# Tokens, attention and last stage in one block, token statistics by groups between the attention steps

## The chip, the cores and the metric

The kernel runs on one core of one Trainium2 chip. Times are device microseconds of one execution; the span of a profile is the time from its first to its last instruction.

## The reference

Three parts follow one another. A graph network makes tokens: three layers over 64 x 64 frames of 75 nodes, then a mean over the nodes. The tokens are joined with 32 text rows per batch, normalised and passed through one attention head with a residual. Then 30 rounds of a small feed-forward step, again with a residual.

```python
h = tok_ref(x, A, W0, ..., v2)                 # 64 batches x 64 tokens x 64
h = concatenate([h, txt], axis=1)              # 64 x 96 x 64
h = h + attn(layernorm(h), Wq, bq, Wk, bk, Wv, bv)
h = h + ffn(layernorm(h), ln_w, ln_b, W, b)    # 30 rounds of the step below

def step(h):
    h = h + 0.01 * tanh(h)
    h = h * sigmoid(h)
    h = layernorm(h) * ln_w + ln_b
    return einsum('bsc,dc->bsd', h, W) + b
```

The `layernorm` outside has no weights: (x - mean) / sqrt(var + 1e-5).

## The kernel before

The program is a row of blocks. Within a block each of the five engines has its own instruction stream, ordered by semaphores; between blocks all engines meet.

`setup` loads parameters and x and prepares constants. `tokenise` runs 205 iterations of five frames in four quarters and leaves the node means in `pooledT`; its last instruction is the VectorE reduction of L700, and SP's queue fetches one iteration's input two iterations ahead (`fetch`, L127).

`fuse` has two blocks. The first is `tokens` (L782). SP loads the text into rows 64 to 95 of `h` (L821). ScalarE issues six loads of weights (L828 to L831), after VectorE has cleared `w4` (L845). VectorE clears further constants (L846 to L851), waits for the text, folds the layer-norm weights into the feed-forward matrix (`fold_weights`, L858 to L872; two small matmuls, L909 and L910, belong to it), and then finishes eight groups of eight batches (`finish`): an add of the bias row from PSUM to `h` (L877) and one statistics instruction per batch (L883). TensorE makes the tokens of a group with eight matmuls (L917) into one of two PSUM banks, so a group waits for the finish of the group two before. After the eighth group the statistics of all 64 batches become a mean and an inverse root together (L894 to L933, with one square root on ScalarE, L833).

The second block holds `attention` and `feed_forward`. Attention has 16 groups of four batches in a pipeline of 20 steps. In step t, in this order:

- TensorE: probabilities times values of group t-4 (L1049), scores of t-2 (L1059), transposes of the probabilities of t-3 (L1068), query, key and value of t-1 (L1077, L1081), transposes of the normalised rows `hn` of t (L1089).
- VectorE: scaled result h2 of t-4 (L1127), maximum of t-2 (L1133), denominator of t-3 (L1137), difference to the maximum `dif` of t-2 (L1144), values of t-1 (L1150), reciprocal of t-3 (L1156).
- GpSimd: centring `hc` (L1028) and scaling `hn` (L1033) of t, one buffer each, then the residual add of t-4 (L1037).
- ScalarE copies between PSUM and SBUF and computes Exp (L1117).

Steps 4 to 9 are a loop, the others are written out. SP stores h2 by groups and reads it back in six chunks of 128 x 512. From step 10 on the engines also prepare the first four chunks for the last stage: statistics on VectorE (`STATS_AT`, L1345, L1348), the inverse root as a power on GpSimd (L1253, called in the same step), centring on GpSimd (`CENTRE_AT`, L1257), scaling on VectorE (`SCALE_AT`, L1357). Chunks 4 and 5 are prepared on VectorE and GpSimd while the last stage opens.

The last stage is software-pipelined over chunks: Tanh and Silu on ScalarE, the update y = x + 0.01 tanh(x), statistics, a power on GpSimd (L1281), scaling `gn` on VectorE (L1394), transposes (L1338) and matmuls (L1323, L1325, L1330) on TensorE.

Of the kernel before, what the change touches and what calls it, by code (L numbers as in the profile page):

```python
# [18 lines left out]
F32 = mybir.dt.float32  # L19
F16 = mybir.dt.float16  # L20
BF16 = mybir.dt.bfloat16
# [60 lines left out]
def build(nc, x_v, txt, AT, A, W0T, W1, W2, par01, par1, par2, weights, out):  # L82
# [10 lines left out]
    with ctx:  # L93
# [14 lines left out]
        pooledT = sb("pooledT", [P, QUART, QF])  # L108
        z_stored = [(sem(f"z_stored_by_sync{k}"), sem(f"z_stored_by_pool{k}")) for k in range(ZK)]
        zst_loaded = [sem(f"z_static_loaded{i}") for i in range(2)]  # L110

        with nc.sbuf_tensor("zp", [P, ZK, 2, 2, PAIRS * HC], F16) as zp:

            setup(nc, ps, x_v, AT, A, W0T, W1, W2, par01, par1, par2, zs, zp, zst, z_stored, zst_loaded,
                  AThi, ATlo, abar, W0K, W1hi, W1lo, W1s, negb1, W2s, b2row, ident)
            tokenise(nc, ps, zs, zst, z_stored, zst_loaded, pooledT, AThi, ATlo, abar, W0K, W1hi, W1lo, W1s, negb1)
        fuse(nc, ps, pooledT, h2_dram, txt, weights, W2s, b2row, ident, out)
# [14 lines left out]
def setup(nc, ps, x_v, AT, A, W0T, W1, W2, par01, par1, par2, zs, zp, zst, z_stored, zst_loaded,  # L132
          AThi, ATlo, abar, W0K, W1hi, W1lo, W1s, negb1, W2s, b2row, ident):

    with ExitStack() as ctx:
# [85 lines left out]
        with nc.Block() as block:  # L221
# [78 lines left out]
            def _(pool):  # L300
# [8 lines left out]
                pool.memset(zst[:], 1.0).then_inc(zst_clear, 1)  # L309
                pool.wait_ge(max_ready, 1)  # L310
# [167 lines left out]
def tokenise(nc, ps, zs, zst, z_stored, zst_loaded, pooledT, AThi, ATlo, abar, W0K, W1hi, W1lo, W1s, negb1):  # L478

    with ExitStack() as ctx:  # L480
# [55 lines left out]
        with nc.Block() as block:  # L536
            @block.sync
            def _(sp):
# [9 lines left out]
                steps(sp, body)  # L548

# [179 lines left out]
def fuse(nc, ps, pooledT, h2_dram, txt, weights, W2s, b2row, ident, out):  # L729

    with ExitStack() as keep:
        def kept(name, shape, dt=F32):
            return keep.enter_context(nc.sbuf_tensor(name, shape, dt))


        w4 = kept("w4", [P, 4, P])
        wq, wk, wv, wf = (w4[:, i, :] for i in range(4))
        wcol = kept("wcol", [P, 4])
        wrow = kept("wrow", [P, 2, D])
# [3 lines left out]
        brow = kept("brow", [P, FW], BF16)  # L743
        h2r = kept("h2r", [P, FCH, FW])
        h2_loaded = keep.enter_context(nc.semaphore("h2_loaded"))
        h = kept("h", [S, B, D])
        mean = kept("mean", [S, B])
        rstd = kept("rstd", [S, B])

        tokens(nc, ps, pooledT, txt, weights, W2s, b2row, ident, w4, wcol, wrow,  # L750
               pct, ones, brow, h, mean, rstd)
        with nc.Block() as block:
            prepare, last_pass = feed_forward(nc, keep, ps, h2r, h2_loaded, ident, wf, pct, ones, brow, out)
# [7 lines left out]
            @block.gpsimd  # L761
            def _(pool):
                attend["gpsimd"](pool, prepare["gpsimd"])
# [8 lines left out]
            def _(act):  # L772
                attend["scalar"](act)
# [3 lines left out]
            def _(dve):  # L777
                attend["vector"](dve, prepare["vector"])
# [3 lines left out]
def tokens(nc, ps, pooledT, txt, weights, W2s, b2row, ident, w4, wcol, wrow,  # L782
           pct, ones, brow, h, mean, rstd):

    W4, w_cols, w_rows = weights
    wf, ln_w, ln_b, bf = w4[:, 3, :], wcol[:, 2:3], wcol[:, 3:4], wrow[:, 1, :]
    v_ = nc.vector
    NT = FRAMES // P
    TG = 4
    BG = 8  # L790
    frames = pooledT[:].rearrange("p q f -> p (q f)")
    with ExitStack() as ctx:
        def sb(name, shape, dt=F32):
            return ctx.enter_context(nc.sbuf_tensor(name, shape, dt))

        def sem(name):
            return ctx.enter_context(nc.semaphore(name))

        halves = sb("halves", [P, P])
        wfT = sb("wfT", [D, D])  # L800
        lbx = sb("lbx", [D, P])
        bres = sb("bres", [P, 2, D])
        bpart = sb("bias_part", [P, D], BF16)
        bs = sb("bn_parts_h", [S, B, 6])
        st = sb("st", [S, 6, B])

        w_clear = sem("w_clear")
        w_loaded = sem("w_loaded")
        txt_loaded = sem("txt_loaded")
        chain = sem("vector_chain2")  # L810
        tok_ready = sem("tok_ready")
        tok_done = sem("tok_done")
        wl_ready = sem("wl_ready")
        mean_ready = sem("mean_ready")
        var_ready = sem("var_ready2")
        root_ready = sem("root_ready2")

        with nc.Block() as block:
            @block.sync
            def _(sp):  # L820
                sp.dma_start(h[T:S], txt.rearrange("b s d -> s b d")).then_inc(txt_loaded, 16)  # L821

            @block.scalar
            def _(act):
                act.wait_ge(w_clear, 1)
                for i in range(2):
                    half = slice(D * i, D * i + D)
                    act.dma_start(w4[half, :, half], W4).then_inc(w_loaded, 16)  # L828
                    act.dma_start(wcol[half, :], w_cols).then_inc(w_loaded, 16)
                act.dma_start(wfT[:], W4[:, 3, :]).then_inc(w_loaded, 16)  # L830
                act.dma_start(wrow[:].rearrange("p i d -> p (i d)"), w_rows.partition_broadcast(P)).then_inc(w_loaded, 16)  # L831
                act.wait_ge(var_ready, 1)
                nc.scalar.activation(st[:, 2, :], st[:, 1, :], ACT.Sqrt).then_inc(root_ready, 1)  # L833

            @block.vector
            def _(dve):
                done = [0]

                def link(ins):
# [611 lines left out]
```

## Time and profile before

| | |
|---|---|
| median of 3 runs | 1688.97 us (1688.37 to 1690.54) |
| the profiled execution | 1689.59 us |
| its span | 1687.8 us |
| busy: TensorE / VectorE / ScalarE / GpSimd | 1570.6 / 1408.3 / 1170.3 / 1348.5 us |
| mean granted TensorE clock | 0.985 of full speed |
| token loop ends | about 1218 us |
| tokens block | 1218 to 1248 us |
| attention | 1248 to 1308 us |
| last stage | to 1681 us, then the last stores |

DVE is VectorE, ACT ScalarE, POOL GpSimd, PE TensorE (PEld its weight loads). Busy times are sums over the span; engines overlap. A granted clock of 1.00 is 2.4 GHz, 0.50 is 1.2 GHz.

### The profile page before, as it was taken

The numbers are of one execution on the slowest core, as the hardware profiler recorded it, in microseconds if no ns is written. First come the engines' busy times: TensorE is split into PE (matmuls) and PEld (weight loads), VectorE is DVE, ScalarE is ACT, GpSimd is POOL, SyncE is SP. The second block draws the span as 40 slices with busy tenths as digits, with TensorE's granted clock in tenths as the row PEclk, the third lists the DMA queues.
The fourth block names the chain that finished last, engine by engine and source line by source line (L and its number), as shares of the span: only waits on it lengthen the run. The fifth ranks groups of instructions, "written<-read, shape, count | busy, mean of one in ns | idle before, by whom it ended". The sixth has DMA issues, their size and how long they took to land. (4 is left out here: it accounts for less than half of the span.)

```text
span 1687.8 us, 64798 instructions
## 1 busy us (share of the span) xinstructions
PE 1570.6 (93%) x22603; PEld 1125.7 (67%) x22603; DVE 1408.3 (83%) x3354; ACT 1170.3 (69%) x2706; POOL 1348.5 (80%) x1500
## 2 busy tenths in 40 slices
PE   8599999999999999999999999999858699999999
PEld 8466666666666666666666666666557588888887
DVE  6388888888888888888888888888767899999998
ACT  3377777777777777777777777777525688888886
POOL 2388888888888888888888888888727788888887
PEclk9999999999999999999999999999979799999999
DMA  5200000000000000000000000000102000000001
GB/s 116 87 7 7 6 7 7 6 7 6 7 6 7 7 6 7 6 7 7 7 7 6 7 6 7 7 6 7 19 5 57 17 0 0 0 0 0 0 0 38
DMA packets 21670, 21.66 MB, mean 13 GB/s; under 512 B 12254, under 2 KB 19342, under 8 KB 21271
## 3 DMA queue, kind: packets, MB, share of 16 engines
q1 hardware_dynamic: 18554, 19.07, 4.3%
q0 software_dynamic: 1120, 1.44, 0.3%
q10 hardware_dynamic: 1972, 0.86, 0.3%
q8 instruction: 13, 0.21, 0.1%
q14 instruction: 11, 0.09, 0.0%
HBM read 14.43 MB, written 6.92 MB: 13 GB/s over the span
## 5 line engine op out<-in xcount | busy, mean ns | idle before, releaser
L693 DVE SCALAR_TENSOR_TENSOR y<-ps,negb,abar 128x375 f32<-128x375 f32 x820 | 477.4, 603 | 129.6 <-PE ps L595 125.2
L649 POOL TENSOR_TENSOR y0lo<-y_whole,y0hi 128x384 f16<-128x384 f32 x410 | 375.0, 915 | 146.1 <-ACT y_whole L625 132.4
L580 PE MATMUL ps<-AThi,y0hi 64*128 64x150 f16 (+1 forms) x4920 | 435.9, 217 | 6.4 <-POOL y0lo L649 4.0
L580 PE MATMUL ps<-AThi,y0lo 64*128 64x150 f16 (+1 forms) x4920 | 436.5, 215 | 0.0
L580 PE MATMUL ps<-ATlo,y0hi 64*128 64x150 f16 (+1 forms) x4920 | 436.2, 215 | 0.0
L624 ACT ACTIVATE y0hi<-ps 128x384 f16<-128x384 f32 x410 | 201.7, 492 | 328.9 <-PE ps L563 324.5
L658 POOL TENSOR_TENSOR y<-y 128x370 f32<-128x370 f32 x410 | 398.1, 971 | 8.3 <-DVE y L693 1.8
L1281 POOL TENSOR_TENSOR rs<-var,expo 128x8 f32<-128x8 f32 x180 | 313.9, 1754 | 50.7 <-DVE var L1348 50.7
L599 PE MATMUL ps<-z_whole,W1s 128*128 128x375 f32 x820 | 340.7, 497 | 0.1
L682 DVE SCALAR_TENSOR_TENSOR y0lo<-ps,y0hi 128x384 f16<-128x384 f32 x410 | 226.5, 553 | 75.2 <-ACT y0hi L626 75.2
L580 PEld LDWEIGHTS ps<-AThi,y0hi 64*128 64x128 f16 x4920 | 259.2, 94 | 21.6 <-issue 11.6
L580 PEld LDWEIGHTS ps<-ATlo,y0hi 64*128 64x128 f16 x4920 | 262.8, 96 | 0.0
L580 PEld LDWEIGHTS ps<-AThi,y0lo 64*128 64x128 f16 x4920 | 260.1, 94 | 0.0
L660 POOL TENSOR_TENSOR y<-y 128x190 f32<-128x190 f32 x410 | 218.0, 532 | 32.2
L687 DVE TENSOR_TENSOR z1lo<-ps,z1hi 128x375 f16<-128x375 f32 x410 | 220.6, 538 | 1.9 <-ACT z1hi L630 1.9
L631 ACT ACTIVATE z_whole<-ps 128x375 f32<-128x375 f32 x410 | 211.4, 516 | 0.0
L630 ACT ACTIVATE z1hi<-ps 128x375 f16<-128x375 f32 x410 | 207.3, 506 | 3.8 <-PE ps L580 3.7
L626 ACT ACTIVATE y0hi<-ps 128x384 f16<-128x384 f32 x410 | 205.2, 500 | 0.0
L625 ACT ACTIVATE y_whole<-ps 128x384 f32<-128x384 f32 x410 | 199.7, 487 | 0.0
L1325 PEld LDWEIGHTS ps<-w,gT 128*128 128x128 f32 x1440 | 190.4, 193 | 6.9
L1325 PE MATMUL ps<-w,gT 128*128 128x128 f32 x1440 | 190.9, 276 | 0.0
L599 PEld LDWEIGHTS ps<-z_whole,W1s 128*128 128x128 f32 x820 | 132.5, 189 | 83.2 <-issue 70.2
(199 smaller groups left out, 2413.6 us busy)
## 6 DMA issues: line engine op xcount, KB each, us to landing
z_static<-z_rows SPq DMA_DIRECT2D x410, 18.0 KB
xs<-in_x_v SPq DMA_DIRECT2D x5, 720.7 KB, 9.1
z_rows<-zp SPq DMA_DIRECT2D x10, 240.0 KB
h_rows<-h SPq DMA_DIRECT2D x16, 96.0 KB, 1.9
h2r<-h_rows SPq DMA_DIRECT2D x6, 256.0 KB, 2.7
out<-h2r SPq DMA_DIRECT2D x6, 256.0 KB, 2.3
z_rows<-zp POOLq DMA_DIRECT2D x5, 240.0 KB, 3.5
h<-in_txt SPq DMA_DIRECT2D x1, 512.0 KB, 4.9
```

Of the source, the lines that this page charges most:

```text
L580: last = nc.tensor.matmul(ps[:, Z1B + 2 * p + j, f0 * V:f0 * V + w], y[rows, par, p, t * C:(t + 1) * C], a[rows, BAND0[t]:BAND0[t] + w], s ...
L599: nc.tensor.matmul(ps[:, Y1B + 1, 0:GV], W1s[:], z1f[:, par, p, :], start=True, stop=True).then_inc(y1_ready[1], 1)
L630: nc.scalar.activation(z1hi[:, par, p, :], ps[:, Z1B + 2 * p, 0:GV], ACT.Identity).then_inc(z1hi_done, 1)
L631: nc.scalar.activation(z1f[:, par, p, :], ps[:, Z1B + 2 * p + 1, 0:GV], ACT.Identity).then_inc(z1f_done, 1)
L649: nc.gpsimd.tensor_tensor(y0lo[:, par, p, 0:HC], y0f[:, p, :], y0hi[:, par, p, 0:HC], ALU.subtract).then_inc(y0lo_by_pool, 1)
L658: nc.gpsimd.tensor_tensor(y[:, :, U1:2 * U1], y[:, :, U1:2 * U1], y[:, :, 0:U1], ALU.add).then_inc(halved, 1)
L660: nc.gpsimd.tensor_tensor(y[:, :, U2:V], y[:, :, U2:V], y[:, :, U1:U2], ALU.add).then_inc(quartered, 1)
L682: nc.vector.scalar_tensor_tensor(y0lo[:, par, p, HC:2 * HC], ps[:, Y0B + 1, 0:HC], 0.0, y0hi[:, par, p, HC:2 * HC], ALU.max, ALU.subtract) ...
L687: nc.vector.tensor_tensor(z1lo[:, par, p, :], ps[:, Z1B + 2 * p, 0:GV], z1hi[:, par, p, :], ALU.subtract).then_inc(z1lo_done, 1)
L693: nc.vector.scalar_tensor_tensor(y1[:, par, 2 * p + i].rearrange("p f v -> p (f v)"), ps[:, Y1B + i, 0:GV], negb1[:, 0:1], abar[:].rearran ...
L1281: nc.gpsimd.tensor_tensor(rs[:, b, :], var[:, b, :], expo[:], ALU.pow).then_inc(rs_done, 1)
L1325: last = nc.tensor.matmul(ps[:, cn, j * P:(j + 1) * P], gT[:, b, j * P:(j + 1) * P], wf, start=False, stop=(j == CP - 1), skip_group_check ...
```

## The change

- The loads of text and weights are issued by SP in the block of the token loop, behind its last fetch (`load_last`). `w4` is cleared by GpSimd in `setup`. `w4`, `wcol`, `wrow`, `wfT` and `h` are allocated for the whole program.
- The block of `tokens` is gone. Its work is handed to the attention block as pieces. TensorE makes groups 0, 1 and 2 ahead, into banks 7, 6 and 5, and the others into bank 7 in front of steps 2, 4, 6, 8 and 10. VectorE finishes groups 0 and 1, folds the weights, and finishes groups 2 to 7 in front of steps 1, 3, 5, 7, 9 and 11. GpSimd takes the power -0.5 of group g in front of step 2g. Constants are cleared by GpSimd; `pct` is made by ScalarE.
- The statistics of a group are four instructions for two batches each in place of eight. The variance stays 64 times as large as before, so the inverse root is 8 times too small; ScalarE multiplies the query, key and value weights by 8 once.
- The 20 steps of attention are all written out.
- The preparation of the last stage moves: statistics in steps 10, 12, 14, 17 (10, 13, 15, 18 before), roots a step later than their statistics, scaling in steps 13, 15, 17 and the fourth in the opening of the last stage; chunks 4 and 5 in its steps 2 and 4 (0 and 2 before).

```diff
+        def load_last(eng):
+            W4, w_cols, w_rows = weights
+            eng.dma_start(h[T:S], txt.rearrange("b s d -> s b d")).then_inc(txt_loaded, 16)
+            eng.wait_ge(w_clear, 1)
+            for i in range(2):
+                half = slice(D * i, D * i + D)
+                eng.dma_start(w4[half, :, half], W4).then_inc(w_loaded, 16)
+                eng.dma_start(wcol[half, :], w_cols).then_inc(w_loaded, 16)
+            eng.dma_start(wfT[:], W4[:, 3, :]).then_inc(w_loaded, 16)
+            eng.dma_start(wrow[:].rearrange("p i d -> p (i d)"), w_rows.partition_broadcast(P)).then_inc(w_loaded, 16)
...
                 pool.memset(zst[:], 1.0).then_inc(zst_clear, 1)
+                pool.memset(w4[:], 0.0).then_inc(w_clear, 1)
                 pool.wait_ge(max_ready, 1)
...
                 steps(sp, body)
+                load_last(sp)
...
+        pairs = kept("bn_pairs_h", [S, B // 2, 6])
+        mean = pairs[:].rearrange("p j (i k) -> p (j i) k", i=2)[:, :, 1]
-        tokens(nc, ps, pooledT, txt, weights, W2s, b2row, ident, w4, wcol, wrow,
-               pct, ones, brow, h, mean, rstd)
...
             def _(pe):
-                attend["tensor"](pe)
+                token["tensor"](pe)
+                attend["tensor"](pe, token["tensor_step"])
                 last_pass["tensor"](pe)
...
+    AHEAD = 3
+    MEANS = (4, 3)
+    def bank(g):
+        return 7 - g if g < AHEAD else 7
+    def make_tokens(pe, g):
+        if g >= AHEAD:
+            pe.wait_ge(tok_done, g if g > AHEAD else 1)
+        for j in range(BG):
+            b = g * BG + j
+            last = nc.tensor.matmul(ps[0:T, bank(g), j * D:(j + 1) * D], frames[:, b * T:(b + 1) * T],
+                                    W2s[:], start=True, stop=True)
+        last.then_inc(tok_ready, 1)
+    def tensor(pe):
+        for g in range(AHEAD):
+            make_tokens(pe, g)
+        pe.wait_ge(wl_ready, 1)
+        pe.wait_ge(filled, 2)
+        nc.tensor.matmul(ps[:, MEANS[0], 0:P], halves[:], wf, start=True, stop=True).then_inc(mean_ready, 1)
+        nc.tensor.matmul(ps[:, MEANS[1], 0:D], lbx[:], wfT[:], start=True, stop=True).then_inc(mean_ready, 1)
+        pe.wait_ge(w_eight, 1)
+    def tensor_step(pe, t):
+        if t == 2:
+            pe.wait_ge(folded, 1)
+            pe.wait_ge(pct_made, 1)
+        if t == 3:
+            pe.wait_ge(tok_done, AHEAD)
+        if t % 2 == 0 and 2 <= t and t // 2 + 2 < NT:
+            make_tokens(pe, t // 2 + 2)
+    def scalar(act):
+        nc.scalar.activation(pct[:], ident[:], ACT.Identity, scale=0.01).then_inc(pct_made, 1)
+        act.wait_ge(w_loaded, NW * 16)
+        nc.scalar.activation(w4[:, 0:3, :], w4[:, 0:3, :], ACT.Identity, scale=D ** 0.5).then_inc(w_eight, 1)
+    def gpsimd(pool):
+        pool.memset(expo[:], -0.5)
+        pool.memset(ones[:], 1.0)
+        pool.memset(brow[:], 0.0)
+        pool.memset(halves[:], 0.0).then_inc(halves_clear, 1)
...
+    def gpsimd_step(pool, t):
+        if t % 2 == 0 and t // 2 < NT:
+            g = t // 2
+            pool.wait_ge(var_ready, g + 1)
+            nc.gpsimd.tensor_tensor(rstd[:, batches(g)], var[:, batches(g)], expo[0:S, 0:BG], ALU.pow).then_inc(rstd_ready, 1)
+            pool.wait_ge(rstd_ready, g + 1)
+    def finish(dve, g):
+        dve.wait_ge(tok_ready, g + 1)
+        v_.tensor_tensor(h[0:T, batches(g), :], ps[0:T, bank(g), :].rearrange("p (b d) -> p b d", b=BG),
+                         b2row[0:T].rearrange("p (one d) -> p one d", one=1).to_broadcast([T, BG, D]),
+                         ALU.add).then_inc(tok_done, 1)
+        dve.wait_ge(tok_done, g + 1)
+        for j in range(g * BG // 2, (g + 1) * BG // 2):
+            last = v_.bn_stats(pairs[:, j, :], h[:, 2 * j:2 * j + 2, :].rearrange("p i d -> p d i"))
+        last.then_inc(bn_made, 1)
+        dve.wait_ge(bn_made, g + 1)
+        v_.tensor_scalar(var[:, batches(g)], square[:, batches(g)], D * EPS, None, ALU.add).then_inc(var_ready, 1)
...
+        dve.wait_ge(txt_loaded, 16)
+        for g in range(2):
+            finish(dve, g)
+        fold_weights()
+    def vector_step(dve, t):
+        if t % 2 == 1 and (t + 3) // 2 < NT:
+            finish(dve, (t + 3) // 2)
...
-    def steps(eng, body, after=None):
-        for t in range(4):
-            body(t, lambda lag, t=t: t - lag >= 0)
-        with eng.Fori(4, 10) as t:
-            body(t, lambda lag: True)
-        for t in range(10, NG + 4):
-            body(t, lambda lag, t=t: t - lag < NG)
+    def steps(eng, body, before=None, after=None):
+        for t in range(NG + 4):
+            if before:
+                before(eng, t)
+            body(t, lambda lag, t=t: 0 <= t - lag < NG)
             if after:
                 after(eng, t)
...
-    STATS_AT, CENTRE_AT, SCALE_AT = (10, 13, 15, 18), (11, 14, 16, 18), (12, 15, 17, 19)
+    STATS_AT, ROOT_AT, CENTRE_AT, SCALE_AT = (10, 12, 14, 17), (11, 13, 15, 18), (12, 14, 16, 18), (13, 15, 17)
     EARLY = len(STATS_AT)
-    LATE_STATS_AT, LATE_SCALE_AT = (0, 2), (1, 4)
+    LATE_STATS_AT, LATE_SCALE_AT = (2, 4), (1, 3, 5)
...
-        if t in STATS_AT:
-            pool_root(pool, STATS_AT.index(t))
+        if t in ROOT_AT:
+            pool_root(pool, ROOT_AT.index(t))
...
-                c = EARLY + LATE_SCALE_AT.index(s)
-                dve.wait_ge(centred[1], c - EARLY + 1)
+                c = EARLY - 1 + LATE_SCALE_AT.index(s)
+                if c < EARLY:
+                    dve.wait_ge(centred[0], c + 1)
+                else:
+                    dve.wait_ge(centred[1], c - EARLY + 1)
                 first_scale(dve, c)
```

## Rows read from the trace of the kernel before

**Rows 1.** Busy us of PE, PEld, DVE, ACT, POOL by stage; granted clock.

```profile
1256.00:1277.00 21.00, 19.53 (x203) 18.40 (x199) 15.44 (x40) 13.73 (x35) 12.17 (x20) 1.00 0.18 37
1277.00:1300.00 23.00, 19.58 (x202) 17.95 (x201) 17.84 (x54) 12.14 (x33) 16.66 (x22) 1.00 0.26 61
1300.00:1324.00 24.00, 7.58 (x54) 6.13 (x54) 20.27 (x62) 11.53 (x21) 17.33 (x13) 0.60 0.19 43
...
1400.00:1600.00 200.00, 200.00 (x1399) 167.49 (x1397) 190.00 (x650) 160.66 (x300) 173.11 (x101) 1.00 0.00 0
```

**Rows 2.** Waits, 1215 to 1325: who <- whom, us, times, longest.

```profile
ACT st L833 <- DVE st L901: 34.2, 1, 34.2
...
POOL rs L1253 <- DVE var L1348: 8.1, 5, 2.2
...
DVE w L858 <- DMA wrow<-in_w_rows: 5.5, 1, 5.5
```

**Rows 3.** Timeline: start us, us, engine, line, instruction, count, [idle before <-releaser].

```profile
33.02 0.42 POOL L311 PARTITION_ALL_REDUCE mxa<-mx  x1 [23.40 <-DVE mx L387]
...
1189.12 7.02 SPq L127 DMA_DIRECT2D z_static<-z_rows  x4
...
1217.52 0.55 DVE L700 TENSOR_REDUCE pooledT<-y 128x20 f32<-128x380 f32 x1 [1.75 <-POOL y L660]
...
1218.39 2.71 PE L917 MATMUL ps<-W2s,pooledT 128*64 128x64 f32 x32 [3.29 <-PEq L536]
...
1225.63 0.29 DVE L858 TENSOR_SCALAR w<-w,wcol 128x128 f32<-128x128 f32 x1 [5.50 <-DMA wrow<-in_w_rows]
...
1227.05 0.69 PE L910 MATMUL ps<-wfT,lbx 64*128 64x64 f32 x2
...
1230.25 0.68 DVE L877 TENSOR_TENSOR h<-ps,b2row 64x512 f32<-64x512 f32 x1
...
1239.60 1.15 PE L917 MATMUL ps<-W2s,pooledT 128*64 128x64 f32 x16 [0.58 <-DVE h L877]
...
1249.36 0.58 PE L1089 MATMUL ps<-ident,hn 96*128 96x96 f32 x2 [8.61 <-POOL hn L1033]
```

**Rows 4.** Groups of instructions, whole span: busy us, mean ns.

```profile
L1345 DVE BATCH_NORM_STATS2 bn_pairs<-h2r 128x6 f32<-128x128 f32 x24 | 5.2, 274 | 0.0
...
L1348 DVE TENSOR_SCALAR var<-bn_pairs 128x8 f32<-128x8 f32 x186 | 31.9, 171 | 6.4
```

**Rows 5.** One source line: duration ns min/median/max, first and last start.

```profile
L1253 POOL TENSOR_TENSOR rs<-var,expo x6: 1643/1670/2017, 1281.4 to 1318.2; 128x8 f32<-128x8 f32 x6
```

**Rows 6.** Groups of instructions in attention steps, 1260 to 1277 us.

```profile
L1037 POOL TENSOR_TENSOR h<-h x6 | 4.3, 724 | 4.3 <-DVE h L1127 4.3
...
L1033 POOL TENSOR_TENSOR hn<-hc,rstd 96x256 f32<-96x256 f32 x6 | 3.7, 609 | 4.2 <-PE ps L1089 4.2
...
L1077 PE MATMUL ps<-hT,w 128*128 128x192 f32 x24 | 5.1, 333 | 0.0
```

**Rows 7.** Timeline, TensorE in attention: step 1; transposes of steps 3, 10, 15.

```profile
1250.36 1.65 PE L1077 MATMUL ps<-hT,w 128*128 128x192 f32 x4 [0.42 <-ACT hT L1110]
...
1259.15 0.33 PE L1089 MATMUL ps<-ident,hn 96*128 96x96 f32 x2
...
1279.59 0.33 PE L1089 MATMUL ps<-ident,hn 96*128 96x96 f32 x2
...
1298.08 0.36 PE L1089 MATMUL ps<-ident,hn 96*128 96x96 f32 x2
```

**Rows 8.** Timeline: a disturbed centring, the last h2, the last stage's opening.

```profile
1288.00 1.17 POOL L1028 TENSOR_TENSOR hc<-h,mean 96x256 f32<-96x256 f32 x1
...
1308.05 0.42 DVE L1127 TENSOR_TENSOR h<-ps,inv 96x256 f32<-96x256 f32 x1 [1.01 <-PE ps L1049]
...
1320.19 0.70 DVE L1394 TENSOR_TENSOR gn<-g,rs 128x512 f32<-128x512 f32 x1
...
1326.79 1.06 PE L1338 MATMUL ps<-ident,gn 128*128 128x128 f32 x4
```

More of the change, by code:

```diff
@@ L777, in _, with tokens @@
             def _(dve):
-                attend["vector"](dve, prepare["vector"])
+                token["vector"](dve)
+                attend["vector"](dve, token["vector_step"], prepare["vector"])
                 last_pass["vector"](dve)
-def tokens(nc, ps, pooledT, txt, weights, W2s, b2row, ident, w4, wcol, wrow,
-           pct, ones, brow, h, mean, rstd):
-    W4, w_cols, w_rows = weights
+def tokens(nc, ctx, ps, pooledT, W2s, b2row, ident, w4, wcol, wrow, wfT, w_loaded, txt_loaded,
+           pct, ones, brow, expo, h, pairs, rstd):
@@ L927, in inverse_root, with sb, sem @@
-def inverse_root(link, v_, root, x, out, tmp):
-    link(v_.reciprocal(out, root))
-    link(v_.tensor_tensor(tmp, out, out, ALU.mult))
-    link(v_.tensor_tensor(tmp, tmp, x, ALU.mult))
-    link(v_.tensor_scalar(tmp, tmp, -0.5, 1.5, ALU.mult, ALU.add))
-    link(v_.tensor_tensor(out, out, tmp, ALU.mult))
+    square = pairs[:].rearrange("p j (i k) -> p (j i) k", i=2)[:, :, 2]
+    def sb(name, shape, dt=F32):
+        return ctx.enter_context(nc.sbuf_tensor(name, shape, dt))
+    def sem(name):
+        return ctx.enter_context(nc.semaphore(name))
@@ new lines, in tokens @@
+    halves = sb("halves", [P, P])
+    lbx = sb("lbx", [D, P])
+    bres = sb("bres", [P, 2, D])
+    bpart = sb("bias_part", [P, D], BF16)
+    var = sb("var64_h", [S, B])
+    chain = sem("vector_chain2")
+    halves_clear = sem("halves_clear")
+    filled = sem("constants_filled")
+    pct_made = sem("pct_made")
+    tok_ready = sem("tok_ready")
+    tok_done = sem("tok_done")
+    bn_made = sem("bn_made_h")
+    var_ready = sem("var_ready2")
+    rstd_ready = sem("rstd_ready")
+    wl_ready = sem("wl_ready")
@@ new lines, in tokens, with batches @@
+    mean_ready = sem("mean_ready")
+    w_eight = sem("w_times_eight")
+    folded = sem("folded")
+    def bank(g):
+        return 7 - g if g < AHEAD else 7
+    def batches(g):
+        return slice(g * BG, (g + 1) * BG)
+    def make_tokens(pe, g):
[6 more added lines that the diff above has]
+        last.then_inc(tok_ready, 1)
@@ new lines, in vector, with link, fold_weights @@
+    def vector(dve):
+        done = [0]
+        def link(ins):
+            done[0] += 1
+            ins.then_inc(chain, 1)
+            dve.wait_ge(chain, done[0])
+        def fold_weights():
+            dve.wait_ge(w_loaded, NW * 16)
+            link(v_.tensor_scalar(wf, wf, ln_w, D ** 0.5, ALU.mult, ALU.mult))
+            v_.tensor_copy(lbx[:], ln_b[0:D].to_broadcast([D, P])).then_inc(wl_ready, 1)
+            dve.wait_ge(mean_ready, 1)
+            link(v_.tensor_tensor(wf, wf, ps[:, MEANS[0], 0:P], ALU.subtract))
+            dve.wait_ge(mean_ready, 2)
+            link(v_.tensor_tensor(bres[:, 0, :], bf, ps[:, MEANS[1], 0:D], ALU.add))
+            dve.wait_ge(filled, 2)
+            for i in range(3):
+                r = slice(32 * i, 32 * i + 1)
+                last = v_.tensor_copy(brow[r, :].rearrange("p (r d) -> p r d", d=D),
+                                      bres[r, i % 2, :].rearrange("p (one d) -> p one d", one=1).to_broadcast([1, FR, D]))
+                if i < 2:
+                    link(v_.tensor_copy(bpart[:], bres[:, i % 2, :]))
+                    link(v_.tensor_tensor(bres[:, 1 - i % 2, :], bres[:, i % 2, :], bpart[:], ALU.subtract))
+            last.then_inc(folded, 1)
+        dve.wait_ge(txt_loaded, 16)
+        for g in range(2):
+            finish(dve, g)
+        fold_weights()
@@ L1091, in body @@
                 last.then_inc(hT_ready, 1)
-        steps(pe, body)
+        steps(pe, body, token)
     def scalar(act):
```

173 lines of the change are left out of this document (35 added, 138 removed).

## The prediction

> **What bounds the kernel now.** I read the busy time by stage first, then the waits around the changed part, then the timeline from the end of the token loop to the last stage, then the cost of single instructions. The stages show that the last stage is TensorE's alone: 200.00 us busy of 200 [rows 1]. The change touches no instruction of it after its opening, and none of the token loop before its last reduction, which ends at 1217.52 + 0.55 = 1218.07 [rows 3]. So whatever is won or lost between 1218 and about 1327 us arrives at the end one for one, and nothing else does.
>
> That stretch has three parts. From 1218.39 (first token matmul) to 1249.36 (first transposes of attention) TensorE mostly waits [rows 3]: for the weights, on which VectorE stands 5.5 us [rows 2]; for their folding, which VectorE does ahead of any token, 1225.63 to 1230.25 [rows 3]; for eight groups of tokens and one inverse root over all of them. From 1249.36 to 1298 attention runs; TensorE is busy 19.53 of 21 us at full clock [rows 1], and a step takes (1279.59 - 1259.15) / 7 = 2.92 us [rows 7]. From 1300 to 1324 TensorE is busy 7.58 of 24 us at a mean granted clock of 0.60 [rows 1], because the last stage opens on VectorE and GpSimd.
>
> **The change part by part.** I follow it on the clock of the old trace. Durations are rows; the schedule laid out of them, with 0.05 to 0.1 us for a wait between engines, is my estimate.
>
> *Loads.* SP's last fetch of the loop is issued by 1189.12 + 7.02 = 1196.1 [rows 3]; the seven loads follow it. Before, the six weight loads were there 1225.63 - 1218.39 = 7.2 us after the block began, so now text and weights lie in SBUF some 10 us ahead of need and the 5.5 us go; without that cover they return whole. Clearing w4 moves to GpSimd in the setup, which then waits 23.40 us anyhow [rows 3]. The small clears took VectorE at most 1225.63 - 5.50 - 1218.39 = 1.7 us; on GpSimd, at up to twice that, they end by 1221.8, about when the first variance is due (below): 0 to 0.2, I take 0. ScalarE's two scalings fall where it waited 34.2 us [rows 2].
>
> *Front, +24.1 us.* TensorE makes groups 0 to 2 at once. Sixteen matmuls took 2.71 us, so 1.36 a group: ready at 1219.75, 1221.1 and 1222.45 [rows 3]. One "finish" is the add, 0.68 [rows 3], four statistics over two batches each, 5.2 / 24 x 4 = 0.87, and a variance, 0.17 [rows 4]: 1.75 with its waits, done at 1221.55 and 1223.2. Folding keeps its 4.6 us, to 1227.8, and finish 2 comes behind it, to 1229.4. On GpSimd the power of group 0 runs from 1221.6 to 1223.3 (1.64 at best, 1.67 at the median [rows 5]); hc and hn, same shape, 0.61 each [rows 6], end at 1224.65. TensorE has first to do the two matmuls on the folded weights, which ended 1227.05 + 0.69 - 1225.63 = 2.1 us after the folding began [rows 3], now at 1225.25. First transposes: 1225.25 instead of 1249.36.
>
> *Steps 0 to 3, -1.3.* The projections of step 1 took 1.65 us [rows 7], against 5.1 / 6 = 0.85 in later steps [rows 6]: the clock was then at 1.2 GHz, its low level. I leave that, and add token group 3 in step 2: 1.0 at full clock (1.15 from first to last end [rows 3]) to 1.36. The wait for the first Exp stays. If the low level lasts through step 2, another 2 us go. Step 3 ends at 1236.65 against 1259.48: 22.8 ahead.
>
> *Steps 4 to 10, -4.1.* Even steps carry a token group (four of them, 4 to 7): 2.92 + 1.0 on TensorE. Odd steps carry a finish on VectorE. In a pair of steps VectorE has 2 x 2.15 (15.44 us in 21 / 2.92 steps [rows 1]) + 1.75 = 6.05 us of 6.85, GpSimd 2 x (0.61 + 0.61 + 0.72) [rows 6] + 1.65 = 5.55. The order holds too: queued behind a finish on VectorE are the step's h2, top, den and dif, and dif still ends about 0.7 us before the scores that wait for it. So only TensorE pays: 4 x 1.03. End of step 10: 1261.3 against 1279.9. The steps that were a loop are now written out, as step 10 was before, which came at the same 2.92: nothing.
>
> *Steps 11 to 15, -2.25.* Before, the early roots of the last stage made GpSimd wait for variances that VectorE had yet to make, 8.1 us over five [rows 2]; two of these hit attention and are most of what its steps 11 to 15 took over 5 x 2.92: 1298.26 - 1279.92 = 18.35 [rows 7]. Now a root stands a step after its statistics and that wait goes. But the roots of steps 11 and 13 run straight into the token powers of steps 12 and 14: 2 x 1.65 + 1.94 = 5.25 us of GpSimd, and a centring besides, against 2.92. What is late next is hn, and TensorE's transposes with it. VectorE adds 0.75 in step 12, where finish 7 follows the first statistics and no token group on TensorE covers it. I lay out 2.9, 6.0, 3.0, 5.5 and 3.2 us: 20.6. End of step 15: 1281.9.
>
> *Tail, +1.1.* Statistics 2 leave step 15, which puts VectorE's chain 0.95 us earlier; a scale and statistics in step 17 weigh about what they did in 17 and 18. Last h2 done: 1291.0 against 1308.47 [rows 8].
>
> *Opening of the last stage, +2.4.* Scale 3, statistics 4 and their centring stood ahead of the first update of x0; now they come behind it. By the same durations the first gn is 8.1 us after the last h2 (1320.19 - 1308.47 = 11.7 before), but from there to the third transposes, where TensorE takes over, it is 7.8 (1326.79 - 1320.19 = 6.6 before [rows 8]), since statistics 4 and 5 and a scale that waits for its Tanh lie between. Third transposes: 1306.9.
>
> Sum: 24.1 - 1.3 - 4.1 - 2.25 + 1.1 + 2.4 = 19.95; by the two ends, 1326.79 - 1306.9 = 19.9. The profiled execution took 1689.59 us, 1.79 more than its span of 1687.8 and 0.6 more than the median of the runs, 1688.97. Off the median: 1669.1 us.
>
> **Weighed against a rule.** Statistics and powers now run side by side. The old trace shows what that can do: hc took 1.17 us at 1288.00 [rows 8], against 0.61, while VectorE ran a scale with two SBUF inputs (L1357), and the slowest root took 2.02, median 1.67 [rows 5]. In the new loop the add reads PSUM and one SBUF row, a statistics instruction one SBUF tile, so the sum has 1.65 and 0.61. The Trainium skill (GPSIMD Engine Reference, Key points) says that GpSimd shares its SBUF interfaces with VectorE and contends with VectorE instructions that have two SBUF inputs or run in a two-port mode. Read narrowly, that spares the finish; if the finish counts after all, rival 1 follows.
>
> **Rivals.** 1: GpSimd becomes the bound of attention. With powers at 2.02 and hc at 1.17 an even step needs 2.02 + 1.17 + 0.61 + 0.72 + 0.2 = 4.7 us against TensorE's 3.95: 0.8 x 4, and 2 x 0.37 + 0.56 = 1.3 in each double step, 5.8 in all: 1674.9. For it speak those two collisions; against it, that most roots took 1.65 beside a busy VectorE.
>
> 2: More is won. If the token matmuls lift the clock before step 1, its projections save 0.8 and its values in proportion 0.4; if GpSimd runs far enough ahead for steps 11 to 15 to cost what they did, 2.25 more: 1665.6. For it, that TensorE now has work in nearly every microsecond from 1218; against it, that hn is a single buffer.
>
> 3: The loads still gate. Landing after 1223 would bring back up to 5.5: 1674.6. Against it the 1196.1.
>
> 4, the other side: TensorE does not get its full clock in attention. It was granted 1.00 with 19.53 of 21 us busy and 0.60 with 7.58 of 24 [rows 1], and the new loop has stalls of 2 to 3 us. A step of 2.92 can become 5.85; seven such steps eat the gain, thirteen give 1669.1 + 38 = 1707. Against it: from 1277 to 1300, with stalls near 2 us, the clock stayed at 1.00 [rows 1].
>
> **How the numbers follow.** Forecast (1666.5 to 1673) 0.62; rival 1, 0.17; rival 2, 0.12; rival 3, 0.03; rival 4, 0.06, of which 0.02 with about seven slow steps, no change, and 0.04 with more. A change of 0.2%, 3.4 us, is about what this measurement can tell. Faster 0.94, same 0.02, slower 0.04. The range holds the forecast, rival 1 whole and most of rival 2: 1664 to 1677.
>
> **What would show it.** Right: no VectorE wait for weights; first transposes about 7 us after the loop's last reduction; steps of 3.9 and 2.9 us by turns; two stalls of TensorE on hn, in steps 12 and 14, over 2 us each with what queues behind; the third transposes of the last stage 16 us after the last h2; its 200 of 200 unchanged. Wrong: a finish over 2 us, powers near 2 us in the loop, TensorE waiting for tok_done or folded, or a granted clock under 1.00 after step 3.

## The result, and the profile after

The changed kernel takes 1669.57 us (median of 4 runs, 1668.63 to 1670.29) against 1689.49 (4 runs, 1688.37 to 1690.54): ratio 0.9882, 95% interval 0.9865 to 0.9899. I had forecast 1669.1. Run again beside other kernels it took 1669.85 against 1689.26, ratio 0.9881 (0.9862 to 0.9901). The total is as forecast. Its terms are not all so, and that is what the experiments are about.

The lines of the kernel moved: the last reduction L700 is now L722, the tokens L917 L855, the add L877 L902, the fold L858 L925, attention's transposes L1089 L1107, h2 L1127 L1145, the first scale L1357 L1370, the update of x0 L1383 L1399, gn L1394 L1410, the last stage's transposes L1338 L1351. The front, on VectorE, in the timeline of the kernel after (start, duration, engine, line; in brackets the idle time before and what ended it), to set beside [rows 3]:

```profile
1215.68 0.55 DVE L722 TENSOR_REDUCE pooledT<-y 128x20 f32<-128x380 f32 x1 [1.76 <-POOL y L682]
1218.60 0.68 DVE L902 TENSOR_TENSOR h<-ps,b2row 64x512 f32<-64x512 f32 x1 [2.38 <-PE ps L855]
...
1222.02 0.28 DVE L925 TENSOR_SCALAR w<-w,wcol 128x128 f32<-128x128 f32 x1
...
1226.42 0.42 DVE L935 CAST brow<-bres 1x512 bf16<-1x512 f32 x1
1226.88 0.68 DVE L902 TENSOR_TENSOR h<-ps,b2row 64x512 f32<-64x512 f32 x1
```

No wait for weights is left. Two finishes take 1.7 us each, the fold 4.8. TensorE in the same part and over two steps, to set beside [rows 7]:

```profile
1216.55 5.35 PE L855 MATMUL ps<-W2s,pooledT 128*64 128x64 f32 x48 [3.30 <-PEq L557]
...
1223.87 0.36 PE L1107 MATMUL ps<-ident,hn 96*128 96x96 f32 x2 [0.41 <-POOL hn L1051]
...
1226.90 1.15 PE L855 MATMUL ps<-W2s,pooledT 128*64 128x64 f32 x16 [0.74 <-DVE brow L935]
...
1234.72 0.33 PE L1107 MATMUL ps<-ident,hn 96*128 96x96 f32 x2
1234.98 1.15 PE L855 MATMUL ps<-W2s,pooledT 128*64 128x64 f32 x16
...
1238.88 0.33 PE L1107 MATMUL ps<-ident,hn 96*128 96x96 f32 x2
...
1241.81 0.33 PE L1107 MATMUL ps<-ident,hn 96*128 96x96 f32 x2
```

The first transposes come 8.19 us after the start of the last reduction (31.84 before), an even step takes 1238.88 - 1234.72 = 4.16 us and an odd one 2.93. The opening of the last stage, to set beside [rows 8], first on VectorE, then on GpSimd, then TensorE's third transposes:

```profile
1289.89 0.42 DVE L1145 TENSOR_TENSOR h<-ps,inv 96x256 f32<-96x256 f32 x1 [0.38 <-PE ps L1067]
1290.60 2.23 DVE L1399 SCALAR_TENSOR_TENSOR x<-th,x 128x512 f32<-128x512 f32 x1 [0.28 <-ACT th L1311]
1292.74 1.21 DVE L1370 SCALAR_TENSOR_TENSOR x<-x,rs 128x512 f32<-128x512 f32 x1
1293.88 0.68 DVE L1399 SCALAR_TENSOR_TENSOR x<-th,x 128x512 f32<-128x512 f32 x1
...
1300.55 0.69 DVE L1410 TENSOR_TENSOR gn<-g,rs 128x512 f32<-128x512 f32 x1
```

```profile
1291.22 1.05 POOL L1273 TENSOR_TENSOR x<-h2r,bn_pairs 128x512 f32<-128x512 f32 x1
1292.23 1.17 POOL L1055 TENSOR_TENSOR h<-h 96x256 f32<-96x256 f32 x1
```

```profile
1308.75 1.12 PE L1351 MATMUL ps<-ident,gn 128*128 128x128 f32 x4 [0.42 <-DVE gn L1410]
```

The first update of x0 took 2.23 us, the next 0.68. The table gives the gain over the profiled execution of before by stretches, for two profiled executions of the changed kernel (spans 1667.5 and 1668.3 against 1687.8). Positive is faster; pct is the constant 0.01 times the identity by which TensorE adds a tanh:

| stretch | forecast | first | second |
|---|---|---|---|
| start to last reduction of the token loop | 0 | 1.84 | 0.89 |
| to the first transposes of attention | 24.1 | 23.65 | 23.65 |
| to those of step 3 | -1.3 | -1.06 | -1.06 |
| to those of step 10 | -4.1 | -4.98 | -4.98 |
| to those of step 15 | -2.25 | -2.40 | -2.72 |
| to the end of the last h2 | 1.1 | 1.11 | 0.94 |
| to the first pct matmul of the last stage (opening) | 2.4 | -0.36 | 0.30 |
| to its last pct matmul | 0 | 2.51 | 2.45 |
| to the end | 0 | -0.01 | -0.01 |

Attention is right within 1 us a row. The opening is wrong by 2.1 to 2.8 us, and the last stage's loop and the start gave 3.3 to 4.4 that I had not forecast. The prediction took the opening to the third transposes: they came 18.44 and 18.31 us after the last h2, against 18.32 before and 15.9 forecast. In the experiments I compare the stretch from the start of the last reduction to the last pct matmul, called **the stretch**: 456.04 us before, 437.57 and 437.46 after.

### The profile page after: what moved, and what is told of

It is laid out like the page before. It is cut to its first block and busy times, and to the rows that moved or that the text cites. A ratio compares the mean times of both kernels' runs of the same rounds, so it can differ in the third digit from the quotient of the medians.

```text
span 1667.5 us, 64566 instructions
## 1 busy us (share of the span) xinstructions
PE 1566.6 (94%) x22603; PEld 1123.6 (67%) x22603; DVE 1407.9 (84%) x3311; ACT 1168.7 (70%) x2707; POOL 1365.7 (82%) x1514
## 5 line engine op out<-in xcount | busy, mean ns | idle before, releaser
L1338 PEld LDWEIGHTS ps<-w,gT 128*128 128x128 f32 x1440 | 190.6, 193 | 6.9
L1338 PE MATMUL ps<-w,gT 128*128 128x128 f32 x1440 | 191.1, 276 | 0.0
```

Of the source, the lines that this page charges most:

```text
L1338: last = nc.tensor.matmul(ps[:, cn, j * P:(j + 1) * P], gT[:, b, j * P:(j + 1) * P], wf, start=False, stop=(j == CP - 1), skip_group_check ...
```

## The experiments

**The loads.** First alone undone, then alone done.

```diff
 steps(sp, body)
-load_last(sp)          # SP, behind the last fetch
...
+load_text(sp)          # SP, start of the last block
...
+load_weights(act)      # ScalarE, start of the last block
```

> The changed kernel with its seven loads back at the start of the last block: text on SP's queue, the six weight loads on ScalarE's, as before the change; everything else as changed. In the kernel before, the weights were there 7.2 us after the block's first matmul (1225.63 against 1218.39). My prediction's step (without the early loads the 5.5 us return whole): VectorE stands 5.5 us ahead of the folding and the kernel takes 1669.6 + 5.5 = 1675.1. Rival: the two finishes that now stand ahead of the folding cover most of the landing; the changed kernel begins to fold 1222.02 - 1216.55 = 5.5 us after its first token matmul, so only 7.2 - 5.5 = 1.7 us come back, 1671.3, with VectorE's wait near 1.7 us.

1674.04 us, the stretch 441.02. VectorE waits 5.11 us, but for the text, at the first finish and not at the fold:

```profile
1222.86 0.68 DVE L907 TENSOR_TENSOR h<-ps,b2row 64x512 f32<-64x512 f32 x1 [5.11 <-DMA h<-in_txt]
```

It would have waited 2.38 us there for tokens anyway, so the first transposes came 10.98 us after the reduction, 2.8 later; steps 1 to 15 took 0.7 to 1.0 us more (58.16 against 57.48 and 57.16). Neither number was right: the front lost 2.8 us, nearer the rival's 1.7 than 5.5, and for the text, of which the rival did not speak.

> The kernel before with one part of the change alone: text and weights are fetched by SP behind the last fetch of the token loop, w4 is cleared by GpSimd in the setup; the block of tokens, its statistics and attention stay. Theory (prediction's step on the loads): VectorE's 5.5 us wait for the weights goes, with the clear of w4 some 0.3 us more, and everything behind it comes that much earlier: first transposes 26.0 us after the start of the loop's last reduction instead of 31.8, and 1690.7 - 5.8 = 1684.9. Rival, from the run with the loads put back (2.8 us later there, not 5.5): the folding in the new place waits for something else that now ends last, the token matmuls or the constants, and only some 3 us are won: 1687.7.

 Its diff is the changed kernel's own hunks on the loads, put into the kernel before.

1685.56 us (0.9973, 0.9960 to 0.9986). The first transposes come 27.54 us after the reduction, 4.3 sooner. The wait for the weights is gone, and the fold waits next for TensorE, which does two token groups before the matmuls of the means:

```profile
1219.64 0.29 DVE L862 TENSOR_TENSOR w<-w,ps 128x128 f32<-128x128 f32 x1 [2.64 <-PE ps L910]
```

So the loads are worth 4.3 us in the front, between my 5.8 and the rival's 3: what they uncovered was 1.75 us more of a wait that had been 0.89. In the profiled execution attention gave 2.9 of it back (62.02 us from the first transposes to the last h2 against 59.12, at a granted clock of 0.65 in the first three steps against 0.78). The median of 12 executions is 3.7 lower.

**The interleaving.**

```diff
-for g in range(AHEAD): make_tokens(pe, g)
+for g in range(NT): make_tokens(pe, g)       # bank 7 - g % 3
...
-for g in range(2): finish(dve, g)
+for g in range(NT): finish(dve, g)           # none in the steps
```

> The changed kernel with all eight token groups made and finished ahead of the folding, none between the steps of attention; the powers stay in their steps. Theory (the value of the interleaving): six more finishes of 1.75 us stand ahead of the folding, so the first transposes come some 10.5 us later, and the five even steps that carried a token group fall back to 2.92 us, 5 x 1.24 = 6.2 us less: 1669.6 + 4.3 = 1673.9. Rival: what the even steps cost is GpSimd's power or VectorE's finish and not TensorE's tokens, so they keep some 4.16 (GpSimd) and the kernel takes 1680; or the front is hidden and nothing is lost, 1670.

1671.56 us, the stretch 439.37: only 1.8 to 1.9 more than the changed kernel. The front lost 10.3 us as expected. Steps 4 to 10 all took 2.92, so the 1.24 of an even step is not GpSimd's power, which stood there still. This run moved VectorE's finishes too; that the 1.24 is TensorE's token group is read from the changed kernel's trace, where TensorE has no wait over 0.25 us from 1234 to 1264 us. Steps 11 to 15 took 19.23 instead of 20.89 and the opening 19.38 instead of 20.5 to 21.2, which I had left out. Of the whole 20 us, making tokens between steps brings 2. The front is 13.35 us shorter than before without it.

**The roots of the last stage.**

```diff
-ROOT_AT, CENTRE_AT, SCALE_AT = (11, 13, 15, 18), (12, 14, 16, 18), (13, 15, 17)
+ROOT_AT, CENTRE_AT, SCALE_AT = (14, 15, 16, 18), (15, 16, 17, 18), (16, 17, 18)
```

> The changed kernel with the roots of the last stage's first chunks in steps 14, 15, 16 and 18 of attention (11, 13, 15, 18 as changed), their centrings in 15, 16, 17, 18 and their scalings in 16, 17, 18. Theory (prediction's step on steps 11 to 15: a root that runs straight into a token power stalls TensorE on hn): steps 11 and 12 fall to 2.9 and about 4, the fall of the granted clock to 0.50 at 1270 goes, and the five steps take 15 to 17.5 us instead of 20.9; the tail may give back up to 2 us, as two roots and three centrings now stand in it; sum 1666 to 1668.5. Rival: the stalls come from VectorE's statistics and finish in these steps, or what is won comes back whole in the tail and the opening of the last stage: 1669.6 or more.

1667.13 us, the stretch 435.72, 1.85 less. Steps 11 to 15 took 16.75 us instead of 20.89, and the tail gave back 2.0. The edit moves centrings and scalings along with the roots. In the changed kernel TensorE waited in steps 12 and 14, first execution:

```profile
1264.00 0.86 PE L1067 MATMUL ps<-val,prT 96*96 96x64 f32 x8 [0.61 <-DVE h L1145]
1265.39 0.59 PE L1077 MATMUL ps<-kT,qT 64*96 64x96 f32 x8 [0.53 <-DVE dif L1162]
...
1269.31 0.38 PE L1107 MATMUL ps<-ident,hn 96*128 96x96 f32 x2 [1.75 <-POOL hn L1051]
...
1278.05 0.39 PE L1107 MATMUL ps<-ident,hn 96*128 96x96 f32 x2 [1.13 <-POOL hn L1051]
```

With the roots late the first two waits stayed, 0.61 and 0.53 us, and those on hn went. Within step 12 the clock fell to its low level. Time by windows, second execution of the changed kernel (busy time and instructions of TensorE, its weight loads, VectorE, ScalarE and GpSimd, then granted clock, DMA share, GB/s):

```profile
1255.00:1268.00 13.00, 11.86 (x120) 10.91 (x121) 11.87 (x39) 6.21 (x17) 8.93 (x11) 0.96 0.22 52
1268.00:1272.00 4.00, 3.58 (x19) 3.07 (x17) 2.54 (x9) 1.63 (x5) 3.84 (x6) 0.50 0.28 68
1272.00:1274.00 2.00, 2.00 (x15) 1.83 (x15) 1.41 (x4) 0.20 (x1) 1.92 (x4) 0.50 0.26 58
1274.00:1278.00 4.00, 4.00 (x27) 3.80 (x26) 2.00 (x6) 1.76 (x5) 3.84 (x4) 0.59 0.12 25
1278.00:1284.00 6.00, 6.00 (x62) 5.64 (x63) 5.86 (x17) 3.80 (x10) 5.49 (x7) 1.00 0.31 72
```

TensorE had 0.50 for 6 us and more, busy nearly throughout; step 13 took 5.50 us (4.53 in the first execution). With the roots late it took 2.97.

**The opening.** The centring of chunk 3 moves to VectorE, behind step 18's instructions.

```diff
-CENTRE_AT = (12, 14, 16, 18)
+CENTRE_AT = (12, 14, 16)
...
+if t == 18: vector_centre(dve, 3)
```

> The changed kernel with the centring of chunk 3 taken from GpSimd (step 18) and given to VectorE in the same step; nothing else. Theory: the first update of x0 took 2.23 us and the scaling behind it 1.21 (0.68 and 0.66 alone) because GpSimd ran the centring of chunk 3 and a residual add beside them, both sides with two inputs in SBUF; without the centring the update falls to 0.7 to 1.2, the centring costs VectorE 0.2 to 0.6 in the tail, and the first gn and the end come 1.0 to 1.4 us earlier: 1668.3. Rival: the update waits for data or is slowed by the transfer of h2, not by GpSimd: it stays near 2.2, and the kernel is 0.2 to 0.6 slower.

1667.97 us. The update is back at its usual length:

```profile
1289.53 0.77 DVE L1369 TENSOR_TENSOR x<-h2r,bn_pairs 128x512 f32<-128x512 f32 x1
1290.22 0.41 DVE L1145 TENSOR_TENSOR h<-ps,inv 96x256 f32<-96x256 f32 x1
1290.69 0.69 DVE L1402 SCALAR_TENSOR_TENSOR x<-th,x 128x512 f32<-128x512 f32 x1
1291.90 1.14 DVE L1375 SCALAR_TENSOR_TENSOR x<-x,rs 128x512 f32<-128x512 f32 x1 [0.52 <-POOL rs L1270]
```

The first gn comes 9.01 us after the last h2 (10.24 and 10.11 in the changed kernel), the third transposes 17.22 us after it (18.44 and 18.31). The stretch, 436.98, is only 0.5 to 0.6 shorter: from the first transposes to the last h2 it took 67.05 us against 66.44 and 66.93, and from the third transposes to the first pct matmul 2.70 against 2.75 and 2.22. Then both edits together, roots as in the run above:

> The changed kernel with both edits: roots in steps 14, 15, 16 and 18, centrings on GpSimd in 15 to 17 and scalings in 16 to 18, and the centring of chunk 3 on VectorE in step 18. Theory: the two gains lie in different places (1.85 us between the loop's end and the last matmuls from the first edit, 1.2 from the last h2 to the first gn from the second) and add: 1669.6 - 3.0 = 1666.5. Rival: with the roots late, VectorE has scalings of its own in the same step, so the second gain is lost again in the tail: 1667.1 or more.

1666.42 us, 3.2 to 3.4 under the changed kernel, as expected. The profiled execution, 1664.19, is the fastest of the four, and its stretch, 432.55, is 5.0 less. The opening takes 18.20 us there where the changed kernel took 21.19 and 20.53. Part of what it has beyond the two gains alone goes with a higher granted clock: from the third transposes to the first pct matmul 1.60 us at a granted 1.00, against 2.31 at 0.68 with the late roots alone and 2.70 at 0.57 with the centring alone; and the first three steps, which neither edit touches, took 10.85 us at 1.00, against 11.71 at 0.73 with the late roots alone. The rest I did not separate.

**The last stage's loop.** The waits from 1400 to 1600 us (engine, tile, line and what it waited for; us, times, longest; "issue" is time in which it waited for nothing that the profile shows), before and after:

```profile
DVE gn L1394 <- issue: 6.5, 17, 0.4
```

```profile
DVE gn L1410 <- issue: 5.0, 17, 0.3
```

That is one wait in each iteration, at the loop's end on VectorE, 0.39 against 0.29 us, and TensorE stands behind it: its pct matmuls are 4.12 us apart there against 4.03, and 3.95 elsewhere in both. The trace has the branch at the loop's end too: the next instruction of VectorE starts 0.27 us after it before, 0.19 us after the change (medians of 28 turns).

```diff
-with eng.Fori(4, 10) as t: ...               # kernel before
+for t in range(NG + 4): body(t, lambda lag, t=t: 0 <= t - lag < NG)
```

> The kernel before with one thing of the change alone: attention's steps 4 to 9, a loop of one step before, are written out. In the changed kernel each iteration of the last stage's loop is 0.09 us shorter on TensorE (4.03 against 4.12 us in the one third of it that holds the loop's end, 3.95 in the other two), some 2.4 us in all, with the same instructions. Theory: that hangs on where the loop's code lies, which this edit moves too: the 4.12 changes (to 4.03 or to another value), and the time by 28 times the difference. Rival: it comes from something else of the change, and the loop keeps its 4.12; the steps of attention keep 2.92 and the time stays within 0.5 us of before, 1689.5.

1691.09 us (1.0000, 0.9992 to 1.0009); 4.12 and 0.39 as before. The rival held, yet the edit had moved the loop little, by 29 of VectorE's records in the trace (19 by the count of the expectations). Two more runs moved it further, each with nothing but clears on VectorE in a wait:

```diff
+for i in range(64): v_.memset(pad[:, i:i + 1], 0.0)    # kernel before; 26 in the changed one
```

> The kernel before with 64 clears of one column of a scratch tile added on VectorE, ahead of its 5.5 us wait for the weights (they take about 64 x 0.07 = 4.5 us of it); nothing reads the tile. In the last stage VectorE stands 0.39 us at each end of its loop ahead of gn, waiting for nothing that the trace shows, against 0.29 in the changed kernel and in the three variants made from it, and 0.39 in the kernel before with attention's steps written out. Counted in VectorE's instructions the loop lies at 469 to 521 and at 488 to 540 in the two with 0.39, and at 443 to 496 in the others, so only the two hold instruction 512. Theory: where the loop's code lies sets its branch back, and a loop across instruction 512 is slower; here it lies at 533 to 585, so 0.29 us, the third of the iteration that holds the loop's end 4.03 us on TensorE instead of 4.12, and 2.4 us less in all: 1688.2 against 1690.6. Rival: it comes from something else that the change brought; the wait stays 0.39, the spacing 4.12 and the time as before, plus what the clears stick out of the wait, 0 to 1 us.

1687.98 us (0.9983, 0.9970 to 0.9997). From the first to the last pct matmul it took 341.74 us, against 344.26 before.

```profile
DVE gn L1397 <- issue: 5.0, 17, 0.3
```

> The changed kernel with 26 such clears on VectorE ahead of its first finish, where it waits 2.4 us for the first tokens, so that its last loop lies at 469 to 521 as in the kernel before. Theory (place of the loop's code): VectorE's wait at the loop's end rises from 0.29 to 0.39 us, the spacing from 4.03 to 4.12, and the kernel is 2.4 us slower, 1672.0. Rival: 0.29, 4.03, and 1669.6.

1672.75 us, and 341.75 turned into 344.25.

```profile
DVE gn L1413 <- issue: 6.6, 17, 0.4
```

The wait goes with the place of VectorE's code, both ways, with no other instruction touched; the branch's 0.27 and 0.19 us change places with it.

**The bias row**, and a sum of all.

```diff
-for i in range(3): ...casts of row i...      # in the fold
+BIAS_AT = (4, 6, 8)                          # one row in each of these steps
```

> The changed kernel with the bias row's nine casts, copies and subtractions (3.0 us of VectorE, 1223.82 to 1226.84), which only the last stage reads, taken out of the folding and done in steps 4, 6 and 8; TensorE waits in step 2 only until the means are read. Theory: in steps 1 and 2 VectorE's queue sets the time (TensorE waited 0.74 us for the fold and 0.91 for val, which stands behind the third finish), so step 3 begins 2 us sooner (10.85 us after the first transposes now), and nothing comes back in steps 4 to 8, where VectorE has 1 us free in each pair: 1669.6 - 2.0 = 1667.6. Rival: the loading of ScalarE's table for the first Exp and the finish are next in the chain, less than 0.7 us is won; or the casts lengthen steps 4, 6 and 8 and eat it.

1671.01 us, the stretch 437.45, the transposes of step 3 after 10.67 us instead of 10.85. The theory fell. TensorE no longer waited for the fold, but its clock was at the low level when the work came, and the token group took 1.90 us instead of 1.15 (windows as above):

```profile
1224.00:1226.00 2.00, 1.34 (x7) 1.15 (x8) 1.89 (x7) 0.33 (x1) 1.84 (x4) 0.89 0.00 0
1226.00:1228.00 2.00, 2.00 (x14) 1.77 (x13) 0.42 (x1) 1.06 (x3) 1.84 (x3) 0.50 0.03 8
1228.00:1230.00 2.00, 2.00 (x22) 1.84 (x21) 0.25 (x1) 0.00 (x0) 1.06 (x2) 0.76 0.00 0
```

The clock is not what keeps the 10.85 us: the changed kernel took them at a granted 1.00 in its first execution and at 0.84, as here, in its second. What ends last in all three is the wait for the first Exp, 1.42 us on TensorE, ahead of which ScalarE loads a table for 1.28 us.

> The changed kernel with the late roots, the centring of chunk 3 on VectorE, the late bias row, and the first statistics of the last stage in step 12 instead of 10 and the second in 13 instead of 12. Theory: in step 12 of the version with both edits TensorE waited for VectorE, which ran the statistics of step 10 and the last finish of step 11 one behind the other (step 4.63 us against 2.92); with the statistics behind the finish 1.2 of these 1.7 us go. With 2 us of the bias row: 1666.4 - 3.2 = 1663.2. Rival: VectorE is short of time in steps 12 and 13 (2.15 + 1.03 us against 2.92) and the stall only moves there, 1664.4; or the bias row brings nothing, 1665.2.

1664.16 us (1662.08 to 1664.34), ratio 0.9845 (0.9828 to 0.9862), against 1669.85 for the changed kernel on the same chip: the fastest here. Its stretch is 432.41, that of the two edits 432.55, so in these two executions the late bias row and the later statistics add nothing: step 12 fell from 4.63 to 3.64 us, and the steps after it and the tail gave that back. By the medians it is 2.3 us faster than the two edits, ratio 0.9845 against 0.9862 (0.9841 to 0.9883); the intervals overlap, and this stays open.

> The changed kernel once more, unaltered, beside the others on one chip. The start of the token loop's last reduction lay between 1215.38 and 1217.52 us in ten profiled executions of kernels that are alike up to there (with and without the change), so this execution's should lie there too, and its distance to the last matmuls of the last stage's loop should be 437.6 again, within 1 us, with 10.85 us from the first to the fourth transposes and 4.03 us at the loop's end. Rival: the 1.84 us by which the changed kernel's loop ended sooner than the one before belong to the change: 1215.7 again, as in the first execution.

1669.85 us; the stretch 437.46, the reduction at 1216.63, first to fourth transposes 10.85.

## Why the prediction was right, and where it was not

**Loads.** The 5.5 us wait went, as said. That it would return whole without the early loads was wrong: 2.8 us came back in the front with the loads put back, since 2.38 of the 5.11 us would have been a wait for tokens anyway.

**Front, +24.1.** Measured 23.65. Finish 1.71, power 1.79 and 1.76 in the first two groups, fold 4.8: near the working. Two of its rows are off. A token group took 5.35 / 3 = 1.78 us instead of 1.36, as the granted clock was at 0.50 from 1215.6 to 1222.4, and in the row of before only from 1219.5 on, so the first finish began 0.7 us later than laid out. And the two matmuls on the folded weights ended where they were laid out, 7.8 us after the start of the reduction, but hn came behind them, at 8.0, and released the transposes.

**Steps 0 to 3, -1.3; 4 to 10, -4.1.** In the first three steps -1.06 was right by its sum: the projections of step 1 ran at full clock in the first execution (0.92 us instead of 1.65), and step 2 took it back in waits for the fold (0.74) and for VectorE's values (0.91). From step 4 on the mechanism (TensorE alone pays for the tokens) is shown by the run with all tokens ahead and the rows above. The size was off: a group costs 1.24 us, not 1.03. Its matmuls take 1.08 (1234.98 to 1236.06, when the next operation starts), the rest goes where it meets the transposes and the next matmuls.

**Steps 11 to 15, -2.25.** Measured -2.40 and -2.72. The stall of step 12 came as laid out (6.25 against 6.0). The late roots took half of it away (4.64, against 2.92 without a stall); what is left there is VectorE, whose statistics and last finish stand one behind the other. Steps 13 and 14 were laid out as 3.0 and 5.5 and came as 4.53 and 4.21, or 5.50 and 3.63. Step 14 has a wait on hn, of 1.13 us, in the first execution alone; the larger part of both is the low clock, rival 4 in small. The sum was right with one half of its cause wrong, by luck. It also took the end of step 15 as 1298.26; by the way it reads steps 3 and 10 it is 1298.08 + 0.36 = 1298.44, and the term -2.1.

**Tail, +1.1.** Measured 1.11 and 0.94.

**Opening, +2.4.** This is the step that failed. "By the same durations the first gn is 8.1 us after the last h2": it came after 10.24 us. The update of x0 took 0.69 us before and 2.23 after, and that is 1.54 of the 2.1. The sentence on hc at 1.17 us in the prediction had the mechanism, and I applied it to attention alone; the opening was where GpSimd's centring and VectorE's updates, with two SBUF operands each, met. There VectorE was the one slowed. The trace of before has that too, in the same place, a scaling beside a residual add:

```profile
1309.82 1.20 DVE L1357 SCALAR_TENSOR_TENSOR x<-x,rs 128x512 f32<-128x512 f32 x1 [1.34 <-POOL x L1257]
```

```profile
1309.74 0.72 POOL L1037 TENSOR_TENSOR h<-h 96x256 f32<-96x256 f32 x1
```

The Trainium skill (GPSIMD Engine Reference, Key points) says that GpSimd contends with VectorE instructions that have two SBUF inputs. The trace agrees, with 2.23 against 0.69 us once the centring was moved. The scaling behind the update stays slow in every kernel here (1.14 to 1.21 us, 0.69 for the next). With both edits the opening takes 18.20 us; 20.83 - 2.4 = 18.4 was the forecast.

**Last stage, 0.** "And nothing else does" was wrong, and "its 200 of 200 unchanged" [rows 1] no proof: TensorE counts as busy for 200.00 of 200 us in both traces, and 2.5 us lay there, at the turn of VectorE's loop.

**Before the change, 0.** The loop's last reduction began between 1214.35 and 1217.52 us in 14 profiled executions: 1216.28 to 1217.52 in the four without early loads, 1214.35 to 1216.79 in the ten with them. The two groups nearly part, 1.1 us in the mean, and 0.8 of it is there at the token loop's first update of y, about 78 us, 1.1 ms ahead of the loads. The clear of w4 in the setup does not part them: the run with the loads put back has it and lies at 1217.21. What does, or whether it is chance, stays open.

**Rivals.** GpSimd did not become the bound up to step 10: powers of 1.63 to 1.79, even steps set by TensorE. Rival 2 (more is won) had its first condition in the first execution, where it brought nothing; what was won came by another way, and the opening took it back, so that 20.3 and 19.5 us of span stand against 19.9 forecast. The total was right by luck: two errors of like size and opposite sign. Of the signs of being wrong that the prediction named, three were there: a finish of 2.12 us (the third), TensorE's wait of 0.74 us for the fold, and a granted clock of 0.50 in steps 12 and 13.

## What to carry to other kernels

Check a forecast by stretches, not by its sum: here some 2.5 us lost in one place and 2.5 won in another cancelled. A collision seen once in a trace (two engines, two SBUF operands each) is to be looked for at every place where the change brings the same pair together. And most of a restructuring's gain may lie in its least conspicuous parts: the interleaving of tokens and attention brought 2 of the 20 us; the loads, the shorter chain ahead of attention and the place of a loop brought the rest.

## What the hardware showed

The place of a loop in an engine's program has a price, 0.10 us at each turn of VectorE's loop. Counted by VectorE's records in the trace, waits, branches and register instructions included and each loop once, the loop lay at 522 to 583, 551 to 612, 532 to 593 and 521 to 582 where a turn had 0.39 us (before, attention written out, 26 clears, loads alone), and at 506 to 567 and 586 to 647 where it had 0.29 (after, 64 clears). So the 512 of the expectations hangs on their count: by this one 512 lies inside a fast loop and inside no slow one. The Trainium skill (Runtime: NRT & Kernel Launch, Instruction fetch mechanics) says that instructions are fetched in blocks of 256 and that a branch out of the blocks at hand stalls for a fetch. The traces list such fetches, packets of 8192 and 16384 bytes on two queues marked as instruction queues, but none, and no other packet, from 1400 to 1600 us in any of these kernels. The runs show the place as the cause; what happens at the branch they do not show.

Where an instruction of GpSimd and one of VectorE with two SBUF inputs met, the slowed one ended about half a microsecond after the other: hc at 1289.17 after the scaling at 1288.71, the first update of x0 at 1292.83 after the centring at 1292.27, and before the change a scaling at 1311.02 after the residual add at 1310.46. That looks as if one ran behind the other; no run tests it.

TensorE's clock was granted at 0.50 (1.2 GHz) from 1270.2 to 1273.6 us in the first execution, after waits of 0.61, 0.53 and 1.75 us in step 12, and from 1267.0 to 1277.2 in the second, after the first two alone. In two kernels alike to the one before up to there (attention's steps written out, and clears added) the mean granted clock of the first three steps was 0.65 against 0.78: from the first transposes to the last h2 these took 61.68 and 61.76 us against 59.11.
